# Set-up, normalising, routing and FFN of a macaron layer as one stage, with the routing of later batches inside the FFN's slots

## The chip, the cores and the metric

One core of a Trainium2 chip runs the program. The metric is the device time of one execution in microseconds (us). Matmuls run on TensorE (PE; its weight loads are shown apart, as PEld), elementwise work on VectorE (DVE), ScalarE (ACT) and GpSimd (POOL); SyncE (SP) issues the transfers.

## What is computed

x has 8 batches of 512 tokens of 128 numbers. Cut to what matters, the reference is:

```python
x = x + 0.5 * ffn(layernorm(x))      # first dense layer
x = x + attention(layernorm(x))      # 16 heads, 128 numbers each, decaying kernel, causal
x = x + 0.5 * ffn(layernorm(x))      # second dense layer, same weights

def ffn(xf):                          # 8 experts, hidden size 176
    scores = softmax(xf @ w_router.T)
    weight, index = top_k(scores, 2)
    h = silu(xf @ w1[e]) * (xf @ w3[e])
    y = h @ w2[e]
    return weight[0] * y[index[0]] + weight[1] * y[index[1]]
```

## The kernel before

All experts are computed for all tokens. 8 x 176 hidden units are 11 groups of 128 (HC = 11), so the FFN of a layer has 8 x 11 = 88 **slots**, a slot being one group of hidden units for one batch of 512 tokens. Each product is done in three passes (`mm3`, L69): operands are split in a high part in a reduced 32-bit format and a low part, and low x high, high x low and high x high are summed.

The program is a row of phases, each a block of its own with a barrier at its end:

- `setup_phase` (L99): loads, the small parameters of the attention (`step` runs operations on VectorE that wait for each other), the moments of x, the products of Wv and Wo per head (`wp`), the split of the FFN's weights in high and low.
- `norm_phase` (L283), three times: the reciprocal root (logarithm and exponential on ScalarE, then a step of refinement on VectorE), the normalised tiles `xn`, their turn by TensorE into `xT`, its high part by ScalarE and its low part by VectorE. Ahead of an FFN (`route`) also the routing: logits of a batch, then for all 32 tiles of 128 tokens at once the softmax and the choice of two (L474 to L496), the turn of the weights into `wT`.
- `ffn_phase` (L503), twice. At the start of a batch a matmul with a constant `selr` spreads the batch's weights into the PSUM bank `w_bank` (L566). In slot e TensorE computes the six matmuls of slot e + 2 (`products`) and then the three of slot e - 1 (`down`); ScalarE takes the SiLU of slot e + 1 and the high part of slot e; VectorE weighs slot e (`hid`, L684, which reads `w_bank` in PSUM and `gated` in SBUF) and gates slot e + 1 (L655); GpSimd makes the low part of slot e (`hid_lo`, L645), both inputs of which lie in SBUF. The first FFN also computes the rotary tables on VectorE and ScalarE: three operations in each of the first slots, one per slot later. After a batch its output is turned back (L588) and added to x (L703).
- `attention_phase` (L749), between the layers.

What orders the work is written by hand: the list of each engine, and semaphores.

## Time and profile before

| | us |
|---|---|
| median of 3 executions | 1844.47 |
| range of these | 1840.91 to 1844.58 |
| the profiled execution | 1838.55 |
| its span | 1836.8 |

| busy, share of the span | |
|---|---|
| TensorE, matmuls | 1681.1 us, 92% |
| VectorE | 1488.8 us, 81% |
| ScalarE | 1434.2 us, 78% |
| GpSimd | 994.2 us, 54% |

The profile is of one execution. A busy time is the sum of an engine's instructions; the records of matmuls overlap, so the distance of their starts says what one costs. In brackets behind an instruction stands how long its engine was idle ahead of it and what ended that. The share of a whole span hides that its stages differ, so stretches are read by themselves.

### The profile page before, as it was taken

To read this page: it belongs to the slowest core of one execution; us is meant where nothing else is said; L and a number is where in the kernel's file an instruction comes from. 1 tells how busy PE (TensorE), PEld (TensorE's weight loads), DVE (VectorE), ACT (ScalarE), POOL (GpSimd) and SP (SyncE) were. 2 spreads that over 40 slices of the span, in tenths; PEclk is the share of its full clock that TensorE was granted. 3 is DMA by queue.
4 is the path that set the end of the run, shared out by engine and by line. 5 is a ranking of instruction groups with operands and counts; after the bars stand their busy time and mean duration, and the time that the engine had idled before them with its cause. 6 is when DMAs were issued, how large, how long until landed. Compare 5 with 4: busy or idle time off the path is not lost. (4 is left out here: it accounts for less than half of the span.)

```text
span 1836.8 us, 30143 instructions
## 1 busy us (share of the span) xinstructions
PE 1681.1 (92%) x9664; PEld 1339.7 (73%) x9664; DVE 1488.8 (81%) x3183; ACT 1434.2 (78%) x2749; POOL 994.2 (54%) x853
## 2 busy tenths in 40 slices
PE   2699995899999999999999999999999999679998
PEld 2478874777777777778778777877777787548886
DVE  6688865889888888988988888898888889656665
ACT  3455575889899898989989899998989988555655
POOL 1166662555555655655565566566566565316665
PEclk8899996999999999999999999999999999879999
DMA  5000011222212222222222222221222212000000
GB/s 158 7 1 1 1 70 41 68 47 72 73 47 73 58 61 56 66 70 50 69 59 63 70 59 64 55 72 47 72 62 57 73 47 58 14 1 7 12 12 18
DMA packets 43261, 92.39 MB, mean 50 GB/s; under 512 B 7392, under 2 KB 19552, under 8 KB 43104
## 3 DMA queue, kind: packets, MB, share of 16 engines
q1 hardware_dynamic: 43104, 90.46, 19.6%
q8 instruction: 78, 1.28, 0.3%
q14 instruction: 79, 0.65, 0.1%
HBM read 18.08 MB, written 5.24 MB: 13 GB/s over the span
## 5 line engine op out<-in xcount | busy, mean ns | idle before, releaser
L1048 POOL TENSOR_TENSOR rot<-by_cos,crossed 128x1024 f32<-128x1024 f32 x128 | 305.3, 2385 | 495.4 <-PE pS L863 268.3
L1056 POOL TENSOR_TENSOR ek<-decay,knorm 128x128 f32<-128x128 f32 (+3 forms) x512 | 431.4, 875 | 32.9 <-ACT knorm L973 32.9
L645 POOL TENSOR_TENSOR hid_lo_f<-hid_f,hid_hi_f 128x512 fp32r<-128x512 f32 x176 | 236.5, 1344 | 221.5 <-ACT hid_hi_f L624 221.3
L965 ACT ACTIVATE z<-z,nmax 128x128 f32<-128x128 f32 (+3 forms) x512 | 281.3, 553 | 87.0 <-DVE nmax L1103 87.0
L1103 DVE CUSTOM_DVE_ANT_0 z<-u,lam,hp 128x128 f32<-128x128 f32 (+3 forms) x512 | 255.8, 556 | 109.7 <-ACT u L993 108.9
L863 PE MATMUL pS<-rot 128*128 128x128 f32 (+3 forms) x1024 | 298.2, 434 | 0.4 <-ACT probT L988 0.4
L981 ACT ACTIVATE u<-u,qnorm 128x128 f32<-128x128 f32 (+3 forms) x512 | 246.1, 551 | 53.2 <-DVE u L1115 48.9
L863 PEld LDWEIGHTS pS<-rot 128*128 128x128 f32 x1024 | 165.4, 192 | 96.1 <-issue 62.1
L1112 DVE SCALAR_TENSOR_TENSOR pS<-pS,ek 128x1280 f32<-128x1280 f32 x128 | 191.6, 1497 | 52.8 <-PE pS L863 52.8
L898 PEld LDWEIGHTS pS<-ident,z 128*128 128x128 f32 x1280 | 141.5, 142 | 83.9 <-ACT z L965 54.1
L898 PE MATMUL pS<-ident,z 128*128 128x128 f32 x1280 | 165.7, 277 | 39.9 <-DVE u L1115 33.2
L1115 DVE TENSOR_TENSOR u<-pS,decay 128x1280 f32<-128x1280 f32 x128 | 190.9, 1491 | 4.4
L876 PEld LDWEIGHTS pV<-ones,squares 128*128 128x128 f32 x1024 | 135.3, 193 | 61.8 <-issue 61.8
L993 ACT ACTIVATE u<-u,hp 128x1280 f32<-128x1280 f32 x128 | 172.6, 1349 | 0.0
L921 PE MATMUL p<-val_odd,probT 128*128 128x128 f32 x1280 | 159.6, 281 | 1.3 <-issue 1.3
L988 ACT ACTIVATE probT<-pS 128x1280 f32<-128x1280 f32 x128 | 156.0, 1219 | 3.1 <-PE pS L898 2.5
L1153 DVE TENSOR_TENSOR by_sin<-pQK,sin 128x1024 f32<-128x1024 f32 x128 | 155.3, 1213 | 3.6 <-PE pQK L73 3.6
L1155 DVE TENSOR_TENSOR by_cos<-pQK,cos 128x1024 f32<-128x1024 f32 x128 | 155.4, 1214 | 0.0
L921 PE MATMUL p<-val_even,probT 128*128 128x128 f32 x1280 | 154.4, 276 | 0.0
L874 PE MATMUL pV<-squares,ones 128*128 128x512 f32 x256 | 134.9, 609 | 21.1 <-ACT squares L999 14.1
L921 PEld LDWEIGHTS p<-val_odd,probT 128*128 128x128 f32 x1280 | 152.1, 196 | 2.8 <-issue 1.4
L624 ACT ACTIVATE hid_hi_f<-hid_f 128x512 fp32r<-128x512 f32 x176 | 111.3, 632 | 50.0 <-DVE hid_f L684 25.3
(230 smaller groups left out, 3522.1 us busy)
## 6 DMA issues: line engine op xcount, KB each, us to landing
crossed<-by_sin SPq DMA_DIRECT2D x256, 256.0 KB, 3.6
cos<-trig_d SPq DMA_DIRECT2D x64, 64.0 KB, 2.1
sin<-trig_d SPq DMA_DIRECT2D x64, 64.0 KB, 2.1
w_raw<-in_w SPq DMA_DIRECT2D x3, 704.0 KB, 7.9
x_sb<-in_x SPq DMA_DIRECT2D x4, 512.0 KB, 6.4
trig_d<-turns_f SPq DMA_DIRECT2D x2, 1024.0 KB, 4.2
wqk_raw<-in_wqk SPq DMA_DIRECT2D x16, 128.0 KB, 3.6
out_x<-x_sb SPq DMA_DIRECT2D x8, 256.0 KB, 2.3
```

What stands on the lines that cost most here:

```text
L645: g.tensor_tensor(hid_lo[:, par], hid[:, par], hid_hi[:, par].bitcast(F32), ALU.subtract).then_inc(lo_done, 1)
L863: last = pe.matmul(s.pS[:, span(I)], rot[:, I * P:(I + 1) * P], rot[:, N:N + (I + 1) * P], start=True, stop=True)
L898: last = pe.transpose(s.pS[:, col:col + P], z[:, col:col + P], s.ident[:])
L921: last = pe.matmul(s.p7[:, I * P:(I + 1) * P], turned[:, OFF[I] + J * P:OFF[I] + (J + 1) * P], val[:, J * P:(J + 1) * P], start=(J == 0), ...
L965: last = a.activation(z[:, span(I)], z[:, span(I)], ACT.Exp, bias=nmax[:, I:I + 1], scale=-1.0, accum_out=rsum[:, r % 4, I:I + 1])
L981: last = a.activation(u[:, span(I)], u[:, span(I)], ACT.Relu, bias=qnorm[:, r % 2, I:I + 1])
L993: a.activation(u[:], u[:], ACT.Ln, bias=hp[par][:, U_MIN:U_MIN + 1]).then_inc(S["ln_done"], 1)
L1048: g.tensor_tensor(rot[:], by_cos[:], crossed[:], ALU.add).then_inc(S["rot_done"], 1)
L1056: last = g.tensor_tensor(ek[:, span(I)], decay[par][:, span(I)], knorm[:, 0:(I + 1) * P], ALU.mult)
L1103: last = v.tensor_tensor_reduce(z[:, span(I)], u[:, span(I)], lam[par][:, near(I)], hp[par][:, NEG_COEF:NEG_COEF + 1], HIGHEST, ALU.add, A ...
L1112: v.scalar_tensor_tensor(s.pS[:, 0:SW], s.pS[:, 0:SW], -2.0, ek[:], ALU.mult, ALU.add).then_inc(S["w_done"], 1)
L1115: v.tensor_tensor(u[:], s.pS[:, 0:SW], decay[par][:], ALU.mult).then_inc(S["t_done"], 1)
```

## The change

`setup_phase`, the three `norm_phase` and the two `ffn_phase` become two calls of one `dense_phase`, one ahead of the attention and one behind. `attention_phase` is the same, word for word.

- **Head.** Only batches 0 and 1 are normalised, turned and routed ahead of the slots.
- **Slots.** Batches 2 to 7 follow within the slots, by tables: `TURN_AT` (two tiles normalised by GpSimd behind the slot two ahead, two behind the slot ahead, then four transposes, high and low), the logits two slots later, the routing of batches 2 to 4 from slot 14 and 5 to 7 from slot 36, each over six slots, the exponential at 15 and 39.
- **Logits** now have the tokens as the stationary operand: 12 matmuls of 8 columns a batch instead of three of 512 and four transposes.
- **Spread.** The weights are copied 16 wide (`wexp`), turned by four transposes and copied by ScalarE to `wb` in SBUF, four batches deep. The matmul with `selr` is gone.
- **First dense stage only.** Moments, roots, parameters, the products of Wv and Wo (`VALUE_AT`), the rotary tables (now with fewer operations) also go into slots; and the turns for the attention (`AGAIN_AT`), whose normalising stage is gone, but for batches 6 and 7 at the end.
- GpSimd splits the FFN's weights, in five pieces.

```diff
-def setup_phase(nc, s):
...
-def norm_phase(nc, s, tag, route):
...
-def ffn_phase(nc, s, tag, last_phase, rotary):
...
+def dense_phase(nc, s, layer):
...
+        g_bank = (s.pS[:, 0:N], s.pQK[:, 0:N])
+        u_bank = (s.pS[:, N:2 * N], s.pQK[:, N:2 * N])
+        y_bank = (s.p6[:], s.p7[:])
+        route_bank, extra_bank = s.pS[:, 2 * N:3 * N], s.p5[:]
+        logits = route_bank[:, 0:GT * NE].rearrange("p (t e) -> p t e", e=NE)
+        SLOTS = B * HC
+        COPY, TURN, ADD, STATS, AGGR = range(1, 6)
+        TURN_AT = {2: 8, 3: 10, 4: 12, 5: 30, 6: 32, 7: 34}
+        ROUTE_AT = (None, 14, 36)
+        EXPAND_AT = {2: 20, 3: 22, 4: 25, 5: 42, 6: 44, 7: 47}
+        SPREAD_AT = {2: 21, 3: 24, 4: 26, 5: 43, 6: 46, 7: 48}
+        EXP_AT = (None, 15, 39)
+        AGAIN_AT = {0: 49, 1: 51, 2: 53, 3: 76, 4: 78, 5: 83} if first else {}
+        VALUE_AT = (16, 26, 55, 62) if first else ()
...
+            def turn_x(j, bank):
+                pe.wait_ge(xn_pool, j + 1)
+                if j < 2:
+                    pe.wait_ge(xn_dve, j + 1)
+                elif j < 2 * B - 1:
+                    pe.wait_ge(xlo_done, j)
+                else:
+                    pe.wait_ge(xn_dve, 3)
+                    pe.wait_ge(wb_copied, B)
+                for q in range(TILES):
+                    last = pe.transpose(bank[:, q * P:(q + 1) * P], xn[:, j % 2, q], s.ident[:])
+                last.then_inc(xt_done, 1)
+            def route(b):
+                g = group_of(b)
+                pe.wait_ge(xlo_done, b + 1)
+                wait(pe, wb_copied, GROUPS[g][0])
+                for q in range(TILES):
+                    toks = slice((b * TILES + q) * P, (b * TILES + q + 1) * P)
+                    last = mm3(pe, logits[:, (b - GROUPS[g][0]) * TILES + q], (s.xT[0][:, toks], s.xT[1][:, toks]),
+                               (s.wr[0][:], s.wr[1][:]), True, True)
+                last.then_inc(logit_done, 1)
+            def spread(b, bank):
+                if b == 0:
+                    pe.wait_ge(wexp_dve, 1)
+                else:
+                    pe.wait_ge(wexp_act, b)
+                if b > 1:
+                    pe.wait_ge(wb_copied, b)
+                for q in range(TILES):
+                    last = pe.transpose(bank[:, q * P:(q + 1) * P],
+                                        wexp[:, b % 2, q].rearrange("p e j -> p (e j)"), s.ident[:])
+                last.then_inc(wb_done, 1)
...
+            def value_turn(g):
+                pe.wait_ge(wvo_in, 32)
...
+            for e in range(SLOTS):
+                c, k = e // HC, e % HC
+                b = at(TURN_AT, e)
+                if b is not None:
+                    wait(pe, wb_copied, 1)
+                    if first:
+                        wait(pe, wp_lo, values_before(e))
+                    turn_x(b, extra_bank)
+                b = at(AGAIN_AT, e)
+                if b is not None:
+                    wait(pe, wp_lo, values_before(e))
+                    turn_x(B + b, extra_bank)
+                b = at(TURN_AT, e - 2)
+                if b is not None:
+                    route(b)
+                b = at(SPREAD_AT, e)
+                if b is not None:
+                    spread(b, route_bank)
+                if e in VALUE_AT:
+                    pe.wait_ge(xlo_done, sum(slot < e for slot in (*TURN_AT.values(), *AGAIN_AT.values())) + 2)
+                    value_turn(VALUE_AT.index(e))
+                if e - 2 in VALUE_AT:
+                    value_product(VALUE_AT.index(e - 2))
+                if e + 2 < SLOTS:
+                    products(e + 2)
+                if e > 0:
+                    down(e - 1)
+                if c > 0 and k == TURN:
+                    turn_y(c - 1)
+            down(SLOTS - 1)
+            turn_y(B - 1)
+            if first:
+                turn_x(B + 6, extra_bank)
+                turn_x(B + 7, route_bank)
...
+            def exponentials(g):
+                n = (GROUPS[g][1] - GROUPS[g][0]) * TILES
+                a.wait_ge(gap_done, g + 1)
+                a.activation(e_s[:, 0:n], gap[:, 0:n], ACT.Exp).then_inc(exp_done, 1)
+            def expand(b):
+                a.wait_ge(w_done, group_of(b) + 1)
+                wait(a, wb_done, b - 1)
+                a.activation(wexp[:, b % 2], w[:, tiles(b, b + 1)].unsqueeze(3).broadcast_to([P, TILES, NE, P // NE]),
+                             ACT.Copy).then_inc(wexp_act, 1)
+            def keep_spread(b, bank):
+                a.wait_ge(wb_done, b + 1)
+                wait(a, hid_done, (b - 3) * HC)
+                a.activation(wb[:, b % 4], bank, ACT.Copy).then_inc(wb_copied, 1)
...
+            for e in range(SLOTS):
+                c, k, par = e // HC, e % HC, e % 2
+                if e + 1 < SLOTS:
+                    do_silu(e + 1)
+                a.wait_ge(hid_done, e + 1)
+                wait(a, y_slot, e - 1)
...
+                b = at(EXPAND_AT, e)
+                if b is not None:
+                    expand(b)
+                b = at(SPREAD_AT, e)
+                if b is not None:
+                    keep_spread(b, route_bank)
+                if first and e == 5:
+                    root(1, 2, B)
+                if e in EXP_AT:
+                    if first and e == EXP_AT[2]:
+                        root(2, 0, 3)
+                    exponentials(EXP_AT.index(e))
+                if first and e == 72:
+                    root(3, 3, 6)
...
+            def normalise(j, q0, q1):
+                b = j % B
+                if q0 == 0 or j < 2:
+                    wait(g, xt_done, j - 1)
+                for q in range(q0, q1):
+                    t = b * TILES + q
+                    last = g.tensor_scalar(xn[:, j % 2, q], s.x_sb[:, t, :], s.mv[:, t, 0:1], rstd[:, t:t + 1],
+                                           ALU.subtract, ALU.mult)
+                if q1 == TILES:
+                    last.then_inc(xn_pool, 1)
...
+                weights_low(0)
+                weights_low(1)
+                weights_low(2)
+                down_low(0)
+                down_low(1)
+            for e in range(SLOTS):
+                par = e % 2
+                g.wait_ge(hi_done, e + 1)
+                wait(g, y_slot, e - 1)
+                g.tensor_tensor(hid_lo[:, par], hid[:, par], hid_hi[:, par].bitcast(F32),
+                                ALU.subtract).then_inc(lo_done, 1)
+                for j0, table in ((0, TURN_AT), (B, AGAIN_AT)):
+                    b = at(table, e + 2)
+                    if b is not None:
+                        if first:
+                            g.wait_ge(rstd_done, 2 if j0 == 0 else 3 + b // 3)
+                        normalise(j0 + b, 0, TILES // 2)
+                    b = at(table, e + 1)
+                    if b is not None:
...
+            def route_gap(g):
+                n = size(g)
+                v.wait_ge(logit_done, GROUPS[g][1])
+                step(v.tensor_reduce(sm[:, 0, 0:n], logits[:, 0:n], AX.X, ALU.max))
+                tt(gap[:, 0:n], logits[:, 0:n], wide(sm[:, 0, 0:n], n), ALU.subtract).then_inc(gap_done, 1)
+                v.wait_ge(gap_done, g + 1)
...
+            def weigh(e):
+                c, k, par = e // HC, e % HC, e % 2
+                if k == 0:
+                    v.wait_ge(wb_copied, c + 1)
+                v.wait_ge(gated_done, e + 1)
+                wait(v, lo_done, e - 1)
+                tt(hid[:, par], wb[:, c % 4], gated[:, par], ALU.mult).then_inc(hid_done, 1)
...
+            route_best(0)
+            prefer(0, size(0))
+            route_rest(0)
+            route_second(0)
+            prefer(1, size(0))
+            route_both(0)
+            route_sum(0)
+            route_weights(0)
+            v.wait_ge(w_done, 1)
+            v.tensor_copy(wexp[:, 0], w[:, tiles(0, 1)].unsqueeze(3).broadcast_to([P, TILES, NE, P // NE])).then_inc(wexp_dve, 1)
+            gate(0)
+            if first:
+                moments(2)
+                moments(3)
+            for e in range(SLOTS):
+                c, k = e // HC, e % HC
+                weigh(e)
+                if e + 1 < SLOTS:
+                    gate(e + 1)
+                if c > 0 and k == ADD:
+                    add_out(c - 1)
+                for g in (1, 2):
+                    if e == ROUTE_AT[g]:
+                        route_gap(g)
+                    if e == ROUTE_AT[g] + 1:
...
+                    if e == ROUTE_AT[g] + 1:
+                        route_best(g)
+                    if e == ROUTE_AT[g] + 2:
+                        prefer(0, size(g))
+                    if e == ROUTE_AT[g] + 3:
+                        route_rest(g)
+                        route_second(g)
+                    if e == ROUTE_AT[g] + 4:
+                        prefer(1, size(g))
+                        route_both(g)
+                        route_sum(g)
+                    if e == ROUTE_AT[g] + 5:
+                        route_weights(g)
+                b = at(TURN_AT, e - 1)
+                if b is not None:
+                    low(b, extra_bank)
+                b = at(AGAIN_AT, e - 1)
+                if b is not None:
+                    low(B + b, extra_bank)
...
-        setup_phase(nc, s)
-        for layer in range(2):
-            with (nc.sbuf_tensor(f"wT{layer}", [P, B * N], F32R) as wT,
-                  nc.sbuf_tensor(f"selr{layer}", [P, P], F32R) as selr):
-                s.wT, s.selr = wT, selr
-                norm_phase(nc, s, f"n{layer}", True)
-                ffn_phase(nc, s, f"f{layer}", layer == 1, layer == 0)
-            if layer == 0:
-                norm_phase(nc, s, "na", False)
-                attention_phase(nc, s)
+        dense_phase(nc, s, 0)
+        attention_phase(nc, s)
+        dense_phase(nc, s, 1)
```

How the lists of the engines move:

**GpSimd, FFN slots.** The first rows are before, second FFN (`hid_lo` is the low part of the hidden units; the number behind x is how often the row stands in a run):

```order
L326 UNCONDITIONAL_BRANCH [waits barrier_Pool_Activation_PE_DVE_SP_gather]
L329 MEMSET wT 128x512 x8
L286 UNCONDITIONAL_BRANCH
L639 UNCONDITIONAL_BRANCH [waits barrier_Pool_Activation_PE_DVE_SP_gather]
L645 TENSOR_TENSOR hid_lo_f<-hid_f,hid_hi_f 128x512 [waits hi_done_f1] x2
L645 TENSOR_TENSOR hid_lo_f<-hid_f,hid_hi_f 128x512 [waits y_slot_f1,hi_done_f1] x86
```

and these are the change, slots 0 to 8 of the second dense stage (`xn` is a normalised tile of 128 tokens, to be turned by TensorE):

```order
L586 TENSOR_TENSOR hid_lo_d<-hid_d,hid_hi_d 128x512 [waits hi_done_d1] x2
L586 TENSOR_TENSOR hid_lo_d<-hid_d,hid_hi_d 128x512 [waits y_slot_d1,hi_done_d1] x5
L544 TENSOR_SCALAR xn_d<-x_sb,mv,rstd_d 128x128 [waits xt_done_d1]
L544 TENSOR_SCALAR xn_d<-x_sb,mv,rstd_d 128x128
L586 TENSOR_TENSOR hid_lo_d<-hid_d,hid_hi_d 128x512 [waits y_slot_d1,hi_done_d1]
L544 TENSOR_SCALAR xn_d<-x_sb,mv,rstd_d 128x128 x2
L586 TENSOR_TENSOR hid_lo_d<-hid_d,hid_hi_d 128x512 [waits y_slot_d1,hi_done_d1]
```

Two of the four tiles of a batch are normalised behind the low part of the slot two ahead of its turn, two behind that of the slot just ahead. Before, GpSimd had nothing but the low parts here.

**VectorE, the same stage, slots 13 to 17.** Before (`hid` is the weighted hidden units, `pV` a PSUM bank with the spread weights, `gated` the gated units):

```order
L684 TENSOR_TENSOR hid_f<-pV,gated_f 128x512 [waits lo_done_f1,gated_done_f1]
L655 TENSOR_TENSOR gated_f<-pQK,silu_f 128x512 [waits silu_done_f1]
L703 TENSOR_TENSOR x_sb<-pV,x_sb 128x512 [waits y_turned_f1]
L684 TENSOR_TENSOR hid_f<-pV,gated_f 128x512 [waits lo_done_f1,gated_done_f1]
L655 TENSOR_TENSOR gated_f<-pS,silu_f 128x512 [waits silu_done_f1]
```

and the change (`wb` is the copy of the spread weights in SBUF, `gap`, `pick`, `sm` are routing tiles):

```order
L713 TENSOR_TENSOR gated_d<-pQK,silu_d 128x512 [waits silu_done_d1]
L726 TENSOR_TENSOR x_sb<-pV,x_sb 128x512 [waits y_turned_d1]
L668 TENSOR_REDUCE sm_d<-pS 128x12 [waits logit_done_d1]
L669 TENSOR_TENSOR gap_d<-pS,sm_d 128x96 [waits dve_d1]
L721 TENSOR_TENSOR hid_d<-wb_d,gated_d 128x512 [waits lo_done_d1,gated_done_d1,gap_done_d1]
L713 TENSOR_TENSOR gated_d<-pS,silu_d 128x512 [waits silu_done_d1]
```

Three slots later, in the same engine's list:

```order
L713 TENSOR_TENSOR gated_d<-pS,silu_d 128x512 [waits silu_done_d1]
L687 SCALAR_TENSOR_TENSOR rest_d<-pick_d,gap_d 128x96
L691 TENSOR_REDUCE sm_d<-rest_d 128x12 [waits dve_d1]
L692 TENSOR_TENSOR pick_d<-rest_d,sm_d 128x96 [waits dve_d1]
L693 TENSOR_TENSOR pick_d<-pick_d,prio 128x96 [waits dve_d1]
L721 TENSOR_TENSOR hid_d<-wb_d,gated_d 128x512 [waits lo_done_d1,gated_done_d1,dve_d1]
L713 TENSOR_TENSOR gated_d<-pQK,silu_d 128x512 [waits silu_done_d1]
L674 TENSOR_REDUCE sm_d<-pick_d 128x12
```

The sum over the weights now stands between slots, in steps that each wait for the one before (`dve_d1`), and `hid` reads two tensors of SBUF where it read one of PSUM and one of SBUF.

**ScalarE, the same stage, slots 15 and 16.** Before it ran these without anything between (`silu`, then `hid_hi`, the high part). The change:

```order
L487 ACTIVATE hid_hi_d<-hid_d 128x512 [waits y_slot_d1,hid_done_d1]
L413 ACT_TABLE_LOAD
L413 ACTIVATE e_s_d<-gap_d 128x96 [waits gap_done_d1]
L390 ACT_TABLE_LOAD [waits gated_done_d1]
L390 ACTIVATE silu_d<-pQK 128x512 [waits guw_done_d1]
L487 ACTIVATE hid_hi_d<-hid_d 128x512 [waits y_slot_d1,hid_done_d1]
```

The exponential of a routing group (`e_s`) has a table load ahead of it and one behind, ahead of the next SiLU. In the first dense stage the list has eleven such loads within the slots (three around each pair of logarithm and exponential that makes a reciprocal root, two around a lone exponential), in the second four.

## Rows read from the trace of the kernel before

**Rows 1.** Table by stretch: engines' busy us (instructions), then granted TensorE clock, DMA share, GB/s.
```profile
0.00:36.70 36.70, 8.36 (x48) 6.92 (x48) 23.83 (x111) 10.57 (x17) 3.37 (x5) 0.94 0.63 196
36.70:75.40 38.70, 21.47 (x120) 13.06 (x120) 22.30 (x55) 19.65 (x42) 4.00 (x8) 0.70 0.01 2
...
1603.00:1641.90 38.90, 21.70 (x120) 13.26 (x120) 22.30 (x55) 19.66 (x41) 4.00 (x8) 0.70 0.01 2
1641.90:1836.80 194.90, 189.02 (x832) 152.94 (x832) 125.79 (x184) 113.65 (x185) 113.94 (x88) 0.99 0.04 12
```

**Rows 2.** Timeline, PE, inside the second FFN: start us, duration us, engine line.
```profile
1820.48 0.40 PE L71 MATMUL p<-hid_hi_f,w_lo 128*128 128x512 f32 x1
...
1821.18 0.40 PE L71 MATMUL pQK<-xT_hi,w_lo 128*128 128x512 f32 x1
```

**Rows 3.** Timeline, the same stretch, ScalarE, VectorE and GpSimd.
```profile
1820.68 0.60 ACT L610 ACTIVATE silu_f<-pS 128x512 f32<-128x512 f32 x1 [0.68 <-PE pS L73]
...
1821.31 0.69 DVE L655 TENSOR_TENSOR gated_f<-pS,silu_f 128x512 f32<-128x512 f32 x1 [0.66 <-ACT silu_f L610]
...
1821.44 0.63 ACT L624 ACTIVATE hid_hi_f<-hid_f 128x512 fp32r<-128x512 f32 x1 [0.16 <-PE p L73]
...
1822.03 0.69 DVE L684 TENSOR_TENSOR hid_f<-pV,gated_f 128x512 f32<-128x512 f32 x1
...
1822.15 1.29 POOL L645 TENSOR_TENSOR hid_lo_f<-hid_f,hid_hi_f 128x512 fp32r<-128x512 f32 x1 [0.77 <-ACT hid_hi_f L624]
```

**Rows 4.** Timeline, PE: first down product of the two FFNs.
```profile
81.62 0.50 PE L71 MATMUL pV<-hid_hi_f,w_lo 128*128 128x512 f32 x1 [0.24 <-POOL hid_lo_f L645]
...
1647.97 0.50 PE L71 MATMUL pV<-hid_hi_f,w_lo 128*128 128x512 f32 x1
```

**Rows 5.** Timeline, VectorE: last residual sum of the two FFNs, start of the attention.
```profile
277.15 0.69 DVE L703 TENSOR_TENSOR x_sb<-p,x_sb 128x512 f32<-128x512 f32 x1 [4.42 <-PE p L588]
...
294.90 0.17 DVE L1074 COPY hp<-params 128x10 f32<-128x10 f32 x1 [0.32 <-PEq L286]
...
1833.35 0.69 DVE L703 TENSOR_TENSOR x_sb<-p,x_sb 128x512 f32<-128x512 f32 x1 [4.42 <-PE p L588]
```

**Rows 6.** Timeline, small steps of the set-up on VectorE, and the moments.
```profile
7.96 0.23 DVE L222 SCALAR_TENSOR_TENSOR sc<-head_in,sc 128x64 f32<-128x64 f32 x1
...
13.58 6.29 DVE L256 BATCH_NORM_STATS2 stats<-x_sb 128x6 f32<-128x128 f32 x32
```

**Rows 7.** Timeline, start of the second normalising stage, ScalarE and PE.
```profile
1603.02 1.28 ACT L384 ACT_TABLE_LOAD   x1 [8.85 <-PEq L754]
1604.32 0.23 ACT L386 ACTIVATE root_n<-var_n 128x32 f32<-128x32 f32 x1
...
1610.62 0.65 PE L71 MATMUL pV<-xT_hi,wr_lo 128*8 128x512 f32 x1
```

**Rows 8.** Timeline, PE: turns back in the FFN; products with one moving column in the attention.
```profile
1814.51 0.60 PE L588 MATMUL pV<-ident,yT_f 128*128 128x128 f32 x4
1814.86 0.47 PE L71 MATMUL pS<-xT_hi,w_lo 128*128 128x512 f32 x1
...
1004.08 0.95 PE L876 MATMUL pV<-ones,squares 128*128 128x1 f32 x8
```

**Rows 9.** Groups by shape, GpSimd: names, shapes, count, busy us, mean ns, idle before.
```profile
L1056 POOL TENSOR_TENSOR ek<-decay,knorm 128x128 f32<-128x128 f32 x128 | 59.1, 462 | 32.9 <-ACT knorm L973 32.9
L1040 POOL TENSOR_SCALAR lam<-lam,hp 128x512 f32<-128x512 f32 x16 | 12.5, 780 | 25.7 <-ACT lam L957 25.7
```

**Rows 10.** Timeline, first FFN, GpSimd and VectorE at 91 and at 128 us.
```profile
91.27 1.33 POOL L645 TENSOR_TENSOR hid_lo_f<-hid_f,hid_hi_f 128x512 fp32r<-128x512 f32 x1 [2.09 <-ACT hid_hi_f L624]
...
91.50 1.65 DVE L672 SCALAR_TENSOR_TENSOR reduced_f<-whole_f,ang_f 128x512 f32<-128x512 f32 x1
...
128.11 0.68 DVE L672 SCALAR_TENSOR_TENSOR reduced_f<-whole_f,reduced_f 128x512 f32<-128x512 f32 x1
...
128.33 1.61 POOL L645 TENSOR_TENSOR hid_lo_f<-hid_f,hid_hi_f 128x512 fp32r<-128x512 f32 x1 [0.24 <-ACT hid_hi_f L624]
```

1047 lines of the change are left out of this document (514 added, 533 removed).

## The prediction

> **What bounds the kernel now.** I read the table by stretch first. The set-up takes 36.7 us with TensorE busy 8.36, each routing stage 38.7 and 38.9 with TensorE busy some 21.5 at a granted clock of 0.70; the second FFN takes 194.9 with TensorE busy 189.0 at 0.99 [rows 1]. So the FFN is TensorE's, and what stands ahead of it is a chain of small steps. The timeline inside the FFN gives the slot: down starts at 1820.48, the next products at 1821.18 [rows 2], so three matmuls cost 0.69 and nine 2.07. In a slot ScalarE works 0.60 + 0.63, VectorE 2 x 0.69, GpSimd 1.29, each with 0.7 to 0.8 idle [rows 3]. The margin to see is that of order: VectorE weighs slot e + 1 from 1822.03, GpSimd starts the low part of slot e at 1822.15 [rows 3]. The low part is ready at 1823.44 and the down product that needs it comes one slot after 1822.5, near 1824.4: about 0.9 us to spare.
>
> **The change part by part**, against the profiled execution, 1838.55 us (span 1836.8), which lies 0.3% under the median of 1844.47; I add the sum to the median.
>
> *Second head.* Before, the stage starts at 1603.02 and the first down product at 1647.97 [rows 4, 7]: 45.0 us. Now: the first logits of a batch came 7.6 after the start [rows 7], with four batches normalised; with two I take 6.3. 24 matmuls of 8 columns: eight with one column take 0.95, some 0.11 each [rows 8] at full clock and twice that at half, which is the clock here: 4.5. Some 17 routing steps of 64 elements at 0.23 and a little wait [rows 6]: 4.3. Weights widened, spread, gated, weighed, high, low: 0.6 + 0.6 + 0.6 + 0.7 + 0.7 + 1.3 and waits, 5.3. Sum 20.4, so **-24.6**.
>
> *First head.* First down product at 81.62 [rows 4]. Now: the small steps of the parameters' first part end at 8.2; moments of two batches are 8 of 32 in 6.29, 1.6 [rows 6]; aggregation 0.6; then a head as above without its table load, 19; moments of two more batches 1.6; and GpSimd's five pieces of weight splitting run just when VectorE makes its routing steps and hold them (below): 4, bounded by 0 and 6. Sum 35.0, so **-46.6**.
>
> *Between first down and last residual sum.* The second FFN takes 1647.97 to 1833.35, 185.4; the first 81.62 to 277.15, 195.5 [rows 4, 5]: the rotary work, three operations a slot at first, cost 10.1, and it is thinned: **-10.1**. TensorE is full here, so what it gets it pays: seven selr matmuls off, -1.6; four transposes take 0.56 from their first start, less the wait [rows 8], 12 small matmuls 1.3; six batches of turn, spread and logits are 6 x (0.56 + 0.56 + 1.3) = 14.5. Second layer **+12.9**; the first has also four value groups of 1.06 and six turns for the attention, 7.6: **+20.5**.
>
> *Turns wait for GpSimd.* TensorE wants the turn at the start of body T, which is 0.97 ahead of the low part of slot T; the low part of slot T - 1 ends 0.2 after that point, and two normalised tiles follow. A tile lies between 0.28 (0.78 for 512 columns scaled like the two-input operation, which takes 0.46 for 128) and 0.46 [rows 9]; I take 0.33. So TensorE stands 0.86 at each of 18 turns, and this is lost, since the low part follows TensorE. With holds (next) it is up to 1.7. I take 1.1, nearer the row without a hold: **+13.2 and +6.6**.
>
> *Holds.* At 91.27 GpSimd starts a low part; a VectorE operation with two SBUF inputs starts at 91.50 and takes 1.65 instead of 0.68, ending 0.55 after GpSimd. At 128 VectorE is first and GpSimd takes 1.61 instead of 1.30 [rows 10]. The two shut each other out. Before, weighing read PSUM; now it reads `wb` in SBUF and is such an operation in each slot. Without other work it starts 0.12 ahead of the low part and wins: low parts take 1.6, inside the 0.9 to spare. With anything between gate and weighing it loses and waits for the low part's end, and a slot becomes 0.55 + 0.04 + 0.63 + 0.08 + 1.29 = 2.6 us instead of 2.07. Some 60 of the first stage's 88 slots and 25 of the second's have such work. Two in a row are free; a longer run costs 0.5 a slot, routing slots 1 more, less what TensorE has extra in the same slots. In full, run by run, I get 26 and 8.6; at the least 0. I take **+12 and +4**, about half, since turns and spreads fall in the same runs.
>
> *Table loads.* A load takes 1.28 and the next activation starts 0.02 after it [rows 7]. Three loads and two short activations are 4.3 behind a high part, where ScalarE has 0.68 idle ahead of a SiLU, 0.16 ahead of a high part and the low part's 0.9, 1.75 in all, before TensorE notices [rows 3]: 2.6 lost, at slots 5, 39 and 72, less where routing stalls anyway: **+6 and +1**. The Trainium skill ("ScalarE: Activation LUTs", section "What ACT_TABLE_LOAD costs") has it that a switch costs a drain of some 1.38 us besides the 1.28. In the trace every load follows a barrier, so none shows a drain; by the page the fifteen loads in slots would cost some 21 us more.
>
> *Rows between the last sum and the attention.* 277.15 to 294.90 is 17.8 [rows 5]. Now: moments, root, refinement, six tiles on GpSimd, one turn, high and low of the last batch, no second pass over four batches: 9.5. **-8.2**.
>
> First layer: -46.6 - 10.1 + 20.5 + 13.2 + 12 + 6 - 8.2 = -13.2. Second: -24.6 + 12.9 + 6.6 + 4 + 1 = -0.1. Sum **-13.3**: 1825.2 for an execution like the profiled one, **1831** on the median. Clock: I cost the half clock only in the heads; the slots stay at full clock while TensorE has no long gap.
>
> **Rivals.**
>
> *No holds (faster).* If weighing and low part do not shut each other out in the slots, the terms go: 4 in the head, 16 in the runs, 18 x 0.24 = 4.3 in the turns. 1831 - 24 = 1807. For it: the low part that had to wait took only 0.31 more, and weighing starts first. Against: both durations of [rows 10]. Chance 0.20.
>
> *Holds in full (the other side: slower).* One mechanism, in the slots of both stages: weighing loses the race to the low part wherever VectorE has work in between. Turns 18 x (1.7 - 1.1) = 10.8, runs 26 + 8.6 - 16 = 18.6: 1831 + 29 = 1860. It decides above the median from the point where runs and turns cost 14 us more than I took, some half of these 29. For it: the durations of [rows 10] and a margin of just 0.12. Against: TensorE's own extra work in the same slots. Chance 0.20.
>
> *Dear table switches.* A drain ahead of each load, as a mechanism of this kernel: ScalarE is in full use ahead of the loads in slots, where all of before's had a barrier ahead. If a load then takes twice its 1.28, fifteen in slots cost 15 x 1.28 = 19 more, nearly all on TensorE since the room of 1.75 is used up: 1850. By the page named above this is what happens. Against: after the load the activation starts at once [rows 7]. Chance 0.07.
>
> **How the numbers follow.** Forecast and its surroundings, 1815 to 1846, get 0.53: of this 0.43 below, 0.06 within and 0.04 above 0.2% of 1844.47 (3.7 us, about what a measurement of this kernel can tell). Faster: 0.43 + 0.20 = 0.63. Same: 0.06 + 0.01. Slower: 0.04 + 0.20 + 0.06 = 0.30. The range for 8 in 10 goes from just under the case without holds, 1804, to just over that with holds in full, 1862; cases of both signs are in it, the likeliest one's own is 1815 to 1846.
>
> **What would show it.** First down product 20 us into the second dense stage and near 35 in the first; if it comes later, routing steps are stretched, and then GpSimd's weight pieces lie beside them. In the slots: TensorE idle ahead of the first transpose of each turn, released by GpSimd's normalised tile, some 1.1 each (0.86 without holds, 1.7 with). The weighing's mean duration: near 0.69 says no holds, near 1.0 says that it loses often; low parts of 1.6 where it wins. ScalarE's gap ahead of a table load within a slot shows a drain or none. TensorE busy near 1.00 between turns in slots 49 to 88 of the second stage, where VectorE has little. The forecast is wrong if weighing stays behind the low part also in slots with nothing between (then every slot is 2.3 or more and both stages are slower), or if the granted clock falls within the slots.

## The result and the profile after

| | before | after |
|---|---|---|
| median, us (fastest to slowest) | 1842.69 (1838.77 to 1844.58) | **1923.45** (1919.38 to 1926.11) |
| ratio after / before | | 1.0439, 95% interval 1.0412 to 1.0467 |
| span of the profiled execution | 1836.8 | 1920.5 |
| mean granted clock of TensorE | 0.971 | 0.964 |

The kernel before ran once more, in 1838.77 us, which moves its median from 1844.47 to 1842.69. The change makes the kernel 81 us slower; 13 us faster were forecast. From the first two parts of the page of after, the rows of TensorE (PE) and of its granted clock:

```profile
PE 1723.0 (90%) x9728; PEld 1364.7 (71%) x9728; DVE 1533.6 (80%) x3152; ACT 1436.5 (75%) x2740; POOL 1095.1 (57%) x935
...
PE   6778787599999999999999999999999999688898
...
PEclk9898998699999999999999999999999999789999
```

TensorE has only 64 small matmuls more than before, yet is busy 1723.0 us where it was 1681.1: some of the same work took longer. The table by stretch of after (columns: stretch, its length, busy time and count of PE, PEld, DVE, ACT and POOL, granted clock, DMA share, GB/s) answers to [rows 1]:

```profile
0.00:36.00 36.00, 18.02 (x64) 14.81 (x65) 22.39 (x86) 13.48 (x24) 14.55 (x14) 0.95 0.68 187
36.00:338.00 302.00, 236.97 (x993) 180.06 (x991) 209.35 (x367) 149.63 (x252) 175.62 (x143) 0.91 0.04 14
338.00:350.00 12.00, 2.23 (x8) 1.43 (x8) 4.65 (x18) 3.01 (x6) 4.73 (x6) 0.50 0.00 0
...
1657.00:1678.00 21.00, 15.72 (x64) 12.83 (x64) 10.21 (x33) 8.28 (x14) 4.15 (x5) 0.67 0.00 0
1678.00:1917.20 239.20, 212.41 (x921) 164.26 (x920) 166.40 (x219) 122.59 (x204) 149.98 (x112) 0.95 0.03 8
```

The heads (what stands ahead of the first down product of a stage) are as short as forecast. The clock of 0.95 in the first one is too high: the trace has no clock record ahead of 27.9 us, and the matmuls of 512 columns at 22 us start 0.43 us apart, each recorded with 0.63, as they do in rows at 0.50. VectorE's first routing step of 128x64, 0.22 elsewhere, is held beside GpSimd's weight pieces:

```profile
22.42 1.99 DVE L683 SCALAR_TENSOR_TENSOR pick_d<-gap_d,prio 128x64 f32<-128x64 f32 x1
...
22.72 0.63 PE L73 MATMUL pS<-xT_hi,w_hi 128*128 128x512 f32 x1
```

The loss is in the two stretches of slots: 302 us where before took 195.5 and 239 where it took 185.4 [rows 4, 5], TensorE with 65 and 27 us of gaps in them. Their ends, on VectorE and TensorE, answer to [rows 4] and [rows 5]:

```profile
338.02 0.69 DVE L726 TENSOR_TENSOR x_sb<-p,x_sb 128x512 f32<-128x512 f32 x1 [5.30 <-PE p L316]
...
350.50 0.17 DVE L1267 COPY hp<-params 128x10 f32<-128x10 f32 x1 [0.33 <-PEq L105]
...
1678.43 0.50 PE L71 MATMUL pV<-hid_hi_d,w_lo 128*128 128x512 f32 x1 [0.20 <-POOL hid_lo_d L586]
```

**A turn.** The timeline of after around the turn of slot 8 in the second dense stage, TensorE, GpSimd and VectorE:

```profile
1691.18 2.51 POOL L544 TENSOR_SCALAR xn_d<-x_sb,mv,rstd_d 128x128 f32<-128x128 f32 x2
...
1693.66 1.26 POOL L586 TENSOR_TENSOR hid_lo_d<-hid_d,hid_hi_d 128x512 fp32r<-128x512 f32 x1
1694.91 2.08 POOL L544 TENSOR_SCALAR xn_d<-x_sb,mv,rstd_d 128x128 f32<-128x128 f32 x2
1695.02 0.69 DVE L721 TENSOR_TENSOR hid_d<-wb_d,gated_d 128x512 f32<-128x512 f32 x1 [1.30 <-POOL hid_lo_d L586]
...
1697.09 1.08 PE L258 MATMUL pV<-ident,xn_d 128*128 128x128 f32 x4 [4.03 <-issue]
...
1698.83 0.63 PE L73 MATMUL pS<-xT_hi,w_hi 128*128 128x512 f32 x1
...
1700.95 0.40 PE L73 MATMUL pV<-hid_hi_d,w_hi 128*128 128x512 f32 x1
```

The first pair of tiles takes GpSimd 2.51 us and puts off the low part of the slot ahead of the turn; the second pair takes 2.08 behind it and ends at 1696.99. TensorE stands 4.03 us and starts 0.10 behind that end, though the view calls the wait "issue"; kernel 1 below shows that it is the tiles. After this gap it runs at half clock (a matmul of 512 columns is recorded with 0.63 us) and is back at 0.40 some 3 us later. The table by stretch has the clock on either side:

```profile
1689.00:1693.00 4.00, 4.00 (x18) 2.78 (x16) 3.35 (x4) 2.33 (x4) 4.00 (x4) 1.00 0.01 2
1697.10:1700.10 3.00, 3.00 (x9) 2.52 (x10) 0.00 (x0) 0.60 (x1) 2.68 (x3) 0.50 0.00 0
1700.50:1703.40 2.90, 2.90 (x13) 2.05 (x11) 2.08 (x3) 1.83 (x3) 1.25 (x1) 1.00 0.00 0
```

**A slot without a turn**, first dense stage, VectorE, ScalarE, GpSimd and TensorE:

```profile
41.21 0.68 DVE L713 TENSOR_TENSOR gated_d<-pS,silu_d 128x512 f32<-128x512 f32 x1
41.32 0.63 ACT L487 ACTIVATE hid_hi_d<-hid_d 128x512 fp32r<-128x512 f32 x1 [1.47 <-DVE hid_d L721]
...
41.81 0.86 DVE L622 BATCH_NORM_STATS2 stats_d<-x_sb 128x6 f32<-128x128 f32 x4
...
42.03 1.29 POOL L586 TENSOR_TENSOR hid_lo_d<-hid_d,hid_hi_d 128x512 fp32r<-128x512 f32 x1 [1.29 <-ACT hid_hi_d L487]
...
42.59 1.28 DVE L721 TENSOR_TENSOR hid_d<-wb_d,gated_d 128x512 f32<-128x512 f32 x1
...
43.47 0.47 PE L71 MATMUL pV<-hid_hi_d,w_lo 128*128 128x512 f32 x1 [0.28 <-POOL hid_lo_d L586]
...
43.90 0.63 ACT L487 ACTIVATE hid_hi_d<-hid_d 128x512 fp32r<-128x512 f32 x1 [1.47 <-DVE hid_d L721]
```

The weighing is issued at 42.59 beside the low part, which ends at 43.32, and is done at 43.87, 0.55 behind it. High part to high part is 43.90 - 41.32 = 2.58 us: 0.63 + 0.08 + 1.29 + 0.55 + 0.03, the 2.6 of the forecast. Counted over the starts of the high part, 2.57 to 2.60 is the commonest slot of the first stage outside turns; in the second one the commonest are 2.07 and a pair of 1.37 and 2.91 (2.14 on average), where the weighing wins every other time. Both groups by line, and the tiles' durations in ns (least, median, most):

```profile
L586 POOL TENSOR_TENSOR hid_lo_d<-hid_d,hid_hi_d 128x512 fp32r<-128x512 f32 x176 | 250.1, 1426 | 227.3 <-ACT hid_hi_d L487 223.5
L721 DVE TENSOR_TENSOR hid_d<-wb_d,gated_d 128x512 f32<-128x512 f32 x176 | 187.5, 1065 | 21.9 <-POOL hid_lo_d L586 17.0 <-ACT wb_d L425 1.5 <-DVE gated_d L713 0.3
...
L544 POOL TENSOR_SCALAR xn_d<-x_sb,mv,rstd_d x86: 782/792/1749, 12.2 to 1785.2; 128x128 f32<-128x128 f32 x86
```

A tile takes GpSimd 0.78 at the least. The forecast had 0.33, and gave 0.46 as the most.

### The profile page after: what moved, and what is told of

Same layout as the page of the kernel before. It is cut to its first block and busy times, and to the rows that moved or that the text cites. A ratio compares the mean times of both kernels' runs of the same rounds, so it can differ in the third digit from the quotient of the medians.

```text
span 1920.5 us, 30350 instructions
## 1 busy us (share of the span) xinstructions
PE 1723.0 (90%) x9728; PEld 1364.7 (71%) x9728; DVE 1533.6 (80%) x3152; ACT 1436.5 (75%) x2740; POOL 1095.1 (57%) x935
## 3 DMA queue, kind: packets, MB, share of 16 engines
q8 instruction: 79, 1.29, 0.3%
## 5 line engine op out<-in xcount | busy, mean ns | idle before, releaser
L586 POOL TENSOR_TENSOR hid_lo_d<-hid_d,hid_hi_d 128x512 fp32r<-128x512 f32 x176 | 250.1, 1426 | 227.3 <-ACT hid_hi_d L487 223.5
L487 ACT ACTIVATE hid_hi_d<-hid_d 128x512 fp32r<-128x512 f32 x176 | 111.2, 632 | 128.8 <-DVE hid_d L721 114.2
L721 DVE TENSOR_TENSOR hid_d<-wb_d,gated_d 128x512 f32<-128x512 f32 x176 | 187.5, 1065 | 21.9 <-POOL hid_lo_d L586 17.0
```

Source lines behind the costliest of these rows:

```text
L586: g.tensor_tensor(hid_lo[:, par], hid[:, par], hid_hi[:, par].bitcast(F32), ALU.subtract).then_inc(lo_done, 1)
L721: tt(hid[:, par], wb[:, c % 4], gated[:, par], ALU.mult).then_inc(hid_done, 1)
```

## Experiments

Kernel 1 is the kernel of experiment 1, and so on. Every time is the median of its run; kernels 8 and 11 ran once, for the durations at their end. The kernel before had medians of 1841.5 to 1841.8 beside them.

**1. The tiles of the slots by VectorE.** GpSimd's calls in the slots go, and VectorE makes all four tiles at the end of its body two slots ahead; the turn waits for them (the lines taken out are GpSimd's, those added VectorE's).

```diff
-                for j0, table in ((0, TURN_AT), (B, AGAIN_AT)):
-                    b = at(table, e + 2)
...
-                        normalise(j0 + b, 0, TILES // 2)
-                    b = at(table, e + 1)
...
-                        normalise(j0 + b, TILES // 2, TILES)
+                    b = at(table, e + 2)
...
+                        wait(v, xt_done, j0 + b - 1)
+                        normalise(j0 + b, 0, TILES)
```

> The four normalised tiles of each turn in the slots are made by VectorE, two slots ahead of the turn, where GpSimd made them one and two slots ahead; all else is the changed kernel's. Theory A (late GpSimd tiles): a tile of 128x128 takes GpSimd 0.78 us, two of them stand behind the low part, and TensorE waits for them; the two slots around a turn take 9 to 11 us in the trace of after where two quiet slots and the turn's own work take about 5.5, so 18 turns x 3.5 = 60 us: 1863 us (1850 to 1875), the waits of TensorE ahead of the turns (L258) under 0.3 us each and GpSimd busy for 18 x 3.1 = 56 us less. Rival B (the low part and the weighing exclude each other): the turns wait for the chain of weighing, high and low part, and not for the tiles; then less than 20 us go: over 1903 us. Rival C (the turns' own work on TensorE and the table loads): no more than 10 us go: over 1913 us.

Measured: 1857.92 us, ratio to before 1.0081 (1.0059 to 1.0104), so 65.5 us less than after. TensorE is idle ahead of the transposes of turns for 36.9 us in all, of which 29.5 belong to the heads and the end (that much is left in kernels 3 and 7, where no turn in a slot waits); after has 83.6. So late tiles cost 54 us of waiting at 18 turns, 3.0 each, of which 7 stay here (0.4 a turn, where under 0.3 were expected), and theory A holds. The 65.5 us are more than the waits that went, 46.7: TensorE is also less at half clock (by the mean granted clock some 85 us of the span, where it was 138); how the rest divides no run shows.

**2. The gated product stays in PSUM.**

```diff
-                wait(pe, gated_done, e - 1)
+                wait(pe, hid_done, e - 1)
                 mm3(pe, u_bank[par], ...
...
-                tt(gated[:, par], u_bank[par], silu[:, par], ALU.mult).then_inc(gated_done, 1)
+                tt(u_bank[par], u_bank[par], silu[:, par], ALU.mult).then_inc(gated_done, 1)
...
-                tt(hid[:, par], wb[:, c % 4], gated[:, par], ALU.mult).then_inc(hid_done, 1)
+                tt(hid[:, par], u_bank[par], wb[:, c % 4], ALU.mult).then_inc(hid_done, 1)
```

> The gated product stays in its PSUM bank (written in place over the up product), so that the weighing reads one tile from PSUM and one from SBUF; the up product two slots later waits for the weighing and no longer for the gating. Theory B: with both inputs in SBUF the weighing can't run beside GpSimd's low part, and weighing (0.6 behind the low part), high part 0.65 and low part 1.3 become one chain of 2.58 us a slot in the quiet slots of the first layer (2.14 on average in the second's) where TensorE needs 2.07; with one input in PSUM the weighing takes 0.69 in every slot and quiet slots go to 2.07: about 50 x 0.5 + 40 x 0.07 = 28 us, 1895 us (1885 to 1905). Rival A' (what is lost is lost at the turns alone): no more than 8 us go, over 1915 us. Rival D: VectorE's gating into PSUM is slower, and the up product waits longer for the weighing: quiet slots stay over 2.3 us, no gain.

Measured: 1873.47 us, ratio 1.0163 (1.0128 to 1.0198), 50.0 less than after: theory B, and nearly twice its size. The groups by line of this kernel:

```profile
L71 PE MATMUL pQK<-xT_hi,w_lo 128*128 128x512 f32 x176 | 73.9, 420 | 17.9 <-DVE hid_d L720 15.1 <-ACT silu_d L389 2.5
...
L585 POOL TENSOR_TENSOR hid_lo_d<-hid_d,hid_hi_d 128x512 fp32r<-128x512 f32 x176 | 229.5, 1304 | 216.4 <-ACT hid_hi_d L486 216.1
...
L720 DVE TENSOR_TENSOR hid_d<-pQK,wb_d 128x512 f32<-128x512 f32 x88 | 60.5, 687 | 2.7 <-POOL hid_lo_d L585 0.4
```

The weighing takes 0.69 instead of 1.07 and the low part 1.30 instead of 1.43; quiet slots are at 2.07. What I had not counted: GpSimd's tiles are no longer held either (mean 0.81 for 0.94), and the turns' waits fall from 54 to 62.2 - 29.5 = 33 us. The edit has a price of its own, since a product two slots later now waits for the weighing: TensorE stands 15.1 us for it ahead of the pQK products and 5.8 ahead of the pS ones, so the 50.0 us are what is left after that.

**3. Both.**

> Both edits together: tiles by VectorE, gated product in PSUM. If A and B are two separate causes, the gains add: 60 + 28 us, 1835 us (1820 to 1850), about the kernel before. If one of them hides behind the other, the sum falls short of the two single gains by over 10 us.

Measured: 1835.57 us, ratio 0.9961 (0.9945 to 0.9977), 87.9 less than after. That it equals the expected 60 + 28 is chance: the single gains were 65.5 and 50.0, and 87.9 is 27.6 short of their sum. So each edit gives something that the other doesn't (tiles by VectorE 65.5 alone and 37.9 on top of kernel 2; the PSUM operand 50.0 alone and 22.4 on top of kernel 1), and part of the loss is gone with either. The durations show one such part, the tiles that the exclusion stretches; that late tiles also push the low part into the weighing is argued.

**4. GpSimd's tiles a slot earlier.** Its two conditions read `e + 3` and `e + 2` where they read `e + 2` and `e + 1`.

> GpSimd still makes the tiles, but each pair a slot earlier (three and two slots ahead of the turn). Theory A says that GpSimd is both late and short of time: the wait for the second pair goes, but a slot with two tiles takes it 1.3 + 1.65 = 2.9 us where TensorE needs 2.07, so 18 turns x 2 slots x 0.85 = 31 us stay of about 60: 1893 us (1880 to 1905). Rival A2 (only late): nearly all goes, 1863 us. Rival A3 (only short of time): nothing goes, 1923 us.

Measured: 1865.77 us, ratio 1.0123 (1.0088 to 1.0157), 57.7 less. The rival "only late" has it: 31 us of GpSimd's own overload do not show. Two reasons, argued and not tested: two slots around a turn also hold 0.60 us of transposes and 1.34 of small products on TensorE, and the holds are still in this kernel, so that most of its slots of the first stage are 2.58 or longer anyway; either gives GpSimd's 2.9 nearly the room that it needs.

**5. The kernel before, its weighing from two SBUF tiles.** The weighing multiplies `gated` by `gated` instead of by the weights' bank; the products are not weighted.

```diff
-                v.tensor_tensor(hid[:, par], w_bank[c % 2], gated[:, par], ALU.mult).then_inc(hid_done, 1)
+                v.tensor_tensor(hid[:, par], gated[:, par], gated[:, par], ALU.mult).then_inc(hid_done, 1)
```

> The kernel before with one thing changed: the weighing reads gated twice (both inputs in SBUF) and not the weights' PSUM bank, so the products are not weighted; all its instructions, waits and orders stay. Theory B (weighing from two SBUF tiles and low part exclude each other): the same longer slots appear in a kernel that has no work of the other batches in its slots: 2.58 us where VectorE has an angle step behind the gating (some 60 slots of the first layer), 2.14 on average elsewhere, so 60 x 0.51 + 100 x 0.07 = 38 us: 1880 us (1865 to 1895). Rival: the exclusion costs only in slots that are full, or the copy of the weights in the changed kernel is what costs: under 8 us, below 1850 us.

Measured: 1877.58 us, ratio 1.0202 (1.0176 to 1.0228): 35.8 us lost by one operand's place.

```profile
L645 POOL TENSOR_TENSOR hid_lo_f<-hid_f,hid_hi_f 128x512 fp32r<-128x512 f32 x176 | 259.2, 1486 | 237.1 <-ACT hid_hi_f L624 234.5 <-PE pV L73 2.6
L684 DVE TENSOR_TENSOR hid_f<-gated_f 128x512 f32<-128x512 f32 x176 | 227.2, 1291 | 27.6 <-POOL hid_lo_f L645 25.4
L624 ACT ACTIVATE hid_hi_f<-hid_f 128x512 fp32r<-128x512 f32 x176 | 111.3, 632 | 163.5 <-DVE hid_f L684 162.0 <-PE pV L73 0.6 <-PE p L73 0.5
```

The weighing goes from 0.69 to 1.29 on average, and ScalarE waits 162.0 us for it, where it waited 25.3 in the kernel before:

```profile
L624 ACT ACTIVATE hid_hi_f<-hid_f 128x512 fp32r<-128x512 f32 x176 | 111.3, 632 | 50.0 <-DVE hid_f L684 25.3 <-PE pV L73 13.8 <-PE p L73 10.5
```

No turn, no routing and no copy of weights stands in these slots, so the exclusion needs none of them.

**6. Eight more pairs of table loads.** To kernel 3, ScalarE gets an `Exp` of a 128x32 tile in eight quiet slots of the second stage.

> e3_both with an Exp of 128x32 on a tile nobody reads in eight quiet slots of the second layer (52, 56, ... 80): each brings a load of the exponential's table and one of Silu's. The sum's way (a pair holds ScalarE for 2 x 1.28 + 0.22 us, less the 0.8 us that ScalarE has free in a slot of 2.07): 8 x 2.0 = 16 us, 1851 us (1847 to 1856). Rival (the page's rule of a drain of 1.38 us with each load): 8 x 4.7 = 38 us, 1873 us. Rival (free time of the slots ahead and behind takes them in): under 4 us.

Measured: 1845.07 us, ratio 1.0014 (1.0004 to 1.0024), 9.5 more than kernel 3: 1.2 us a pair, under the 2.0 and just under the range that were expected, and far from the 4.7 of a drain. ScalarE around one of them:

```profile
1753.54 0.63 ACT L492 ACTIVATE hid_hi_d<-hid_d 128x512 fp32r<-128x512 f32 x1 [0.16 <-PE pV L73]
1754.18 1.28 ACT L510 ACT_TABLE_LOAD   x1
1755.48 0.23 ACT L510 ACTIVATE price_d<-rstd_d 128x32 f32<-128x32 f32 x1
1755.71 1.28 ACT L395 ACT_TABLE_LOAD   x1
1757.01 0.60 ACT L395 ACTIVATE silu_d<-pS 128x512 f32<-128x512 f32 x1
```

Each load starts when the operation ahead ends and is 1.28 long: no drain beside it. The slots around it are 3.96, 1.60 and 1.78 long: the first loses 1.89 against 2.07, and the two behind it win back 0.76, which the expectation left out. The drain of some 1.38 us that the Trainium skill ("ScalarE: Activation LUTs", section "What ACT_TABLE_LOAD costs") states is not in this kernel.

**7. The small steps ahead of the gating.** In kernel 3 the steps of routing and of the head parameters move from behind `gate(e + 1)` to between `weigh(e)` and `gate(e + 1)`, where GpSimd is idle while ScalarE makes the high part.

```diff
                 weigh(e)
+                for g in (1, 2):
+                    if e == ROUTE_AT[g]:
+                        route_gap(g)
...
                 if e + 1 < SLOTS:
                     gate(e + 1)
-                for g in (1, 2):
-                    if e == ROUTE_AT[g]:
-                        route_gap(g)
...
```

> e3_both with the small steps of routing and of the head parameters standing ahead of the next gating on VectorE, so right behind the weighing, in the 0.65 us in which ScalarE makes the high part and GpSimd does nothing. Theory E (what is left of the slot stretches 14 to 19 and 36 to 42 is held steps: the first small step issued while the low part runs ends only with it, 1.0 to 1.3 us for 0.2): 4 groups x 5 steps x 0.8 = 16 us less, 1820 us (1812 to 1828), and the mean of those steps falls from about 1.2 to 0.3 us. Rival F (the number of steps and the table load set these slots): within 3 us of 1835.6. Rival G (the later gating makes the silu and the up product wait): slower, over 1840 us.

Measured: 1821.6 us, ratio 0.9887 (0.9869 to 0.9904), 14.0 less than kernel 3. Two of the steps in the groups by shape, first of kernel 3, then of this one:

```profile
L670 DVE TENSOR_TENSOR pick_d<-pick_d,sm_d 128x96 f32<-128x96 f32 x8 | 9.7, 1213 | 0.3
L703 DVE TENSOR_TENSOR w_d<-e_s_d,pick_d 128x96 f32<-128x96 f32 x4 | 5.4, 1344 | 0.1
```
```profile
L670 DVE TENSOR_TENSOR pick_d<-pick_d,sm_d 128x96 f32<-128x96 f32 x8 | 2.3, 288 | 0.3
...
L703 DVE TENSOR_TENSOR w_d<-e_s_d,pick_d 128x96 f32<-128x96 f32 x4 | 1.0, 258 | 0.1
```

Same operation, same shape, 1.2 to 1.3 us in one place and 0.26 to 0.29 in the other. In kernel 3 each of the twelve starts while a low part runs and ends 0.11 or 0.12 us behind its end.

**8. Prices of GpSimd, alone.** 24 operations at the very end of after's kernel.

> The changed kernel with 24 operations of GpSimd at the very end, alone there: four each of tensor_scalar 128x128 with two per-partition scalars, with two constants, with one per-partition scalar, with one constant, then two each of 128x512 with two per-partition scalars and with two constants, then four tensor_tensor 128x128. If the price of a tile lies in the loading of per-partition scalars, those with constants take about 0.3 us and 128x512 with constants about 0.8; if it is a fixed price of a tensor_scalar on GpSimd, all four of 128x128 take about 0.78; tensor_tensor 128x128 about 0.46 as in the trace of before. The time grows by some 12 to 18 us at the end.

```profile
1917.80 3.12 POOL L613 TENSOR_SCALAR scratch_d<-xn_d,mv,rstd_d 128x128 f32<-128x128 f32 x4
1920.89 2.47 POOL L615 TENSOR_SCALAR scratch_d<-xn_d 128x128 f32<-128x128 f32 x4
1923.34 2.34 POOL L617 TENSOR_SCALAR scratch_d<-xn_d,mv 128x128 f32<-128x128 f32 x4
1925.66 2.01 POOL L619 TENSOR_SCALAR scratch_d<-xn_d 128x128 f32<-128x128 f32 x4
1927.66 4.13 POOL L621 TENSOR_SCALAR scratch_d<-xn_d,mv,rstd_d 128x512 f32<-128x512 f32 x2
...
1935.54 1.69 POOL L625 TENSOR_TENSOR scratch_d<-xn_d 128x128 f32<-128x128 f32 x4
```

Both theories of a tile's price fell; the two-input operation is as in [rows 9]. Constants for pointers (operands read per partition) save only 0.16 us a tile (0.78 to 0.62), and 128x512 takes 2.07, not the 0.78 of [rows 9]. One difference was left to that row: it multiplies and adds, all of these subtract. After's own rotary steps on GpSimd, which have constants, point the same way: 128x512 with one subtraction 1.77 us, as multiply and add 0.70.

**9. The tile as multiply and add.**

```diff
-                    last = g.tensor_scalar(xn[:, j % 2, q], s.x_sb[:, t, :], s.mv[:, t, 0:1], rstd[:, t:t + 1],
-                                           ALU.subtract, ALU.mult)
+                    last = g.tensor_scalar(xn[:, j % 2, q], s.x_sb[:, t, :], rstd[:, t:t + 1], shift[:, t:t + 1],
+                                           ALU.mult, ALU.add)
```

> The changed kernel, its tiles still made by GpSimd at the same places, but as x times rstd plus shift (shift = minus mean times rstd, one more small step of VectorE per group of roots) where it was x minus mean times rstd. Theory H (on GpSimd a tensor_scalar whose first operation is a subtraction is the slow form: 1.77 us for 128x512 with a subtraction and 0.70 for multiply and add in the same trace, 0.78 in the attention stage; so the prediction's 0.33 us a tile was read from a row of another operation): a tile takes 0.3 us alone, the pair behind the low part 0.65 for 1.65, and of the 65 us that late tiles cost, 20 stay, as the prediction had them: 1880 us (1868 to 1892). Rival (a tile of 128x128 costs 0.78 by its size and its pointers, whatever the operation): no change, 1923 us.

Measured: 1887.47 us, ratio 1.0247 (1.0231 to 1.0263), 36.0 less than after, within the expected range, but 7 short of its middle: the pair behind a low part takes 1.31 us on average, not 0.65, and the turns still wait 62.8 - 27.4 = 35 us (the heads and the end, with cheaper tiles, wait 27.4, as in kernel 10).

**10. All together:** tiles by GpSimd as multiply and add and a slot earlier (for the first turn of the first stage, whose roots come late, both pairs two slots ahead), gated product in PSUM, small steps first.

> All that was learnt together: tiles by GpSimd as multiply and add and a slot earlier, gated product in PSUM, small steps ahead of the gating. Against e7_steps_first (1821.6 us), where VectorE makes the tiles: VectorE is 4 x 0.28 us a turn shorter, but TensorE already works without a gap around most turns there, so 0 to 8 us less: 1817 us (1811 to 1824). If GpSimd's tiles still cost 0.78 us, over 1835 us.

Measured: **1808.9 us, ratio 0.9822 (0.9808 to 0.9836)**, 1.8% under the kernel before and 114.6 us under after; 2 us better than the edge of what was expected. No turn in a slot waits. Its stretches of slots in the table by stretch:

```profile
32.60:260.00 227.40, 212.80 (x997) 169.99 (x996) 172.60 (x383) 151.64 (x253) 147.07 (x144) 0.98 0.07 22
...
1600.00:1807.10 207.10, 197.79 (x925) 159.67 (x923) 136.04 (x219) 124.25 (x205) 123.49 (x112) 0.99 0.04 11
```

The same matmuls keep TensorE busy 1683.0 us in this kernel and 1723.0 in after, 40 more. The half clock explains most of these 40 and not all. At half clock no more than half of the time is lost: in the slots of after that is 302.0 x 0.09 + 239.2 x 0.05 = 39 us, here 227.4 x 0.02 + 207.1 x 0.01 = 7, so at most 32 come from the clock. What the rest is, no run shows; records of matmuls overlap, and after's row of matmuls is broken some 45 times more often, so more of their ends stand uncovered in the sum.

**11. Prices again, by operation:** 18 operations at the end of kernel 9.

> e9_mult_add with 18 operations of GpSimd at the very end, alone there, all with two per-partition scalars: four tiles of 128x128 each as multiply and add, add and multiply, subtract and multiply; then one of 128x512 of each; then tensor_tensor 128x512 as add, subtract and multiply. Theory H: 0.3 us each for multiply and add against 0.78 for subtract and multiply, and 0.78 against 2.07 at 128x512; which of the two the form add and multiply follows tells whether it is the subtraction or the order. The tensor_tensor forms all take 1.27. Rival: all tiles take 0.78.

The durations in ns (least, median, most) of the twelve tiles, and of the three of 128x512:

```profile
L615 POOL TENSOR_SCALAR scratch_d<-xn_d,mv,rstd_d x12: 447/448/797, 1878.0 to 1883.7; 128x128 f32<-128x128 f32 x12
...
L617 POOL TENSOR_SCALAR scratch_d<-xn_d,mv,rstd_d x3: 767/768/2072, 1884.5 to 1886.0; 128x512 f32<-128x512 f32 x3
```

In order of time these are four tiles each and then one row of 512 each as multiply and add, add and multiply, subtract and multiply. Multiply and add or add and multiply: 0.45 a tile, 0.77 for 128x512. Subtract and multiply: 0.80 and 2.07. So it is the subtraction and not whether the addition comes first or second; a subtraction as second operation was not tried. A tensor_tensor of 128x512 takes 1.26, whether it adds, subtracts or multiplies. The 0.3 us of the expectation was too low for a tile as multiply and add as well.

## Why the prediction was wrong

The forecast was 1831 us with 1804 to 1862 as its range; 1923 lies 61 us outside. Against the profiled execution the overrun is 1920.5 - (1836.8 - 13.3) = 97 us:

| part | forecast | measured |
|---|---|---|
| first down product, first / second stage, from its start | 35.0 / 20.4 | 36.0 / 21.1 |
| first down to last sum, first stage | 237.1 | 302.0 |
| the same, second stage | 209.9 | 238.7 |
| last sum to attention | 9.5 | 12.5 |

The rows add up to 98; the attention and the rounding take 1 of it back.

**The heads were right**, within 1 us each, with the half clock and the held steps in them. In the second one the terms measured 7.0, 5.3, 4.1 and 4.7 us where 6.3, 4.5, 4.3 and 5.3 stood in the sum, so each was near and they partly cancel; in the first one three held steps cost 4.2 where 4 was taken. The rows ahead of the attention ran 3 us over, of which 2.8 are six tiles at 0.79 instead of 0.33.

**The step that failed first is the price of a tile.** "A tile lies between 0.28 (0.78 for 512 columns scaled ...) and 0.46 [rows 9]; I take 0.33." The 0.78 was of a multiply and add. The tile subtracts first, and that form takes 0.78 for 128 columns (kernels 8, 11). Both bounds were bounds of another operation. Even for a multiply and add, 0.33 was low: it takes 0.45 (kernel 11), since the row was scaled like the two-input operation (1.29 at 512 columns, 0.46 at 128), and this one shrinks less (0.77 and 0.45). Making the tile a multiply and add gives 36.0 us (kernel 9).

**The second is how tiles reach TensorE.** "TensorE stands 0.86 at each of 18 turns", 1.1 taken, 19.8 us in all; it was 3.0 each and 54 us. The working counted the pair behind the low part of slot T - 1. It left out the pair ahead of that low part, on the same engine: GpSimd has some 0.78 us free in a slot, and 1.6 to 2.7 us of tiles put off the low part, and with it the second pair. Kernel 9 shows that the price alone does not mend it (35 us stay), kernel 4 that starting a slot earlier does, at the full price (9.9 us stay of 54, and the kernel is 57.7 faster).

**The third is a state, not a term.** "The slots stay at full clock while TensorE has no long gap" was the condition, and the turns made most of the long gaps: 4.03 us at 1697, then half clock for 3. The granted clock was 0.91 and 0.95 in the two stretches, and this is worth up to 39 us, 32 more than in kernel 10; it stood nowhere in the sum. Not every turn is followed by half clock, and three such stretches of the first stage stand behind table loads instead (at 52, 182 and 287 us); that the forecast is wrong "if the granted clock falls within the slots" did stand in the text.

**The holds were right in kind and too small.** "Holds in full" ended at 1860 and had the right side. Its mechanism is shown from both ends: put into the kernel before it costs 35.8 us (kernel 5), taken from after it gives 50.0 (kernel 2), or 22.4 where the tiles are no longer late (from kernel 1 to kernel 3), against the 16 of the runs in the forecast, and the weighing's mean of 1.07 is the sign that the text named. What failed is "Two in a row are free; a longer run costs 0.5 a slot ... I take +12 and +4". A slot that has lost stays lost: once the weighing starts behind the low part, the next high part, low part and weighing are late by the same amount, and the slots run at 2.58 for as long as VectorE has anything between. Small routing steps were held too, "routing slots 1 more" in the forecast's words; their place is worth 14.0 us, measured on kernel 3 (kernel 7).

**Table loads**: +7 forecast. The three slots with a root take 5.62, 5.66 and 5.49 us in kernel 3, some 3.5 over a quiet one where 2.6 was reckoned, but single pairs cost 1.2 (kernel 6). What all fifteen cost together no run shows. The rival of dear switches is out: each of the fifteen starts 0.02 us behind the operation ahead, and the next operation starts 0.01 to 0.12 behind its end.

**What the idea was worth.** With the holds, the tiles and their order put right, slots that carry the other batches' routing give 1808.9 us, below the 1831 of the forecast. That this is near the 1807 of the rival without holds is chance: that sum kept 15.5 us of waits at turns, and it did not have the new place of the small steps.

The parts do not add exactly, since they feed each other (kernels 1 to 3); how the 92 us between the two medians divide is known only to that extent.

## What to carry to other kernels

Price an operation from a row with the same engine, shape and the same arithmetic; where the operation differs, its row bounds nothing. When work is put into slots, add up each helper engine's time slot by slot and follow its queue: what stands ahead of the critical operation counts as much as what stands behind it, and a gap on TensorE costs more than its length where the clock falls behind it. Before an operand moves from PSUM to SBUF, look at what GpSimd does at that moment; and put small VectorE steps where GpSimd is idle.
